# A GRU scan ahead of a mixture of experts: ScalarE makes s(1-z), VectorE's products and states become plain two-operand operations, and four instruction lists change

## The reference

```
def cell(h, x):
    gi = x @ W_ih + b_ih
    gh = h @ W_hh + b_hh
    i_r, i_z, i_n = jnp.split(gi, 3, axis=-1)
    h_r, h_z, h_n = jnp.split(gh, 3, axis=-1)
    r = jax.nn.sigmoid(i_r + h_r)
    z = jax.nn.sigmoid(i_z + h_z)
    n = jnp.tanh(i_n + r * h_n)
    h_new = (1.0 - z) * n + z * h
    return (h_new, h_new)
...
logits = flat_x @ Wg + bg
top_vals, top_idx = jax.lax.top_k(logits, TOPK)
...
for i in range(E):
    ...
    h = jax.nn.gelu(tok @ W1[i], approximate=False)
    y = h @ W2[i] * p
    out = out.at[sel_idx].add(y)
```

## Time and profile before

| | |
|---|---|
| median of 3 runs | 836.57 us (836.47 to 837.41) |
| the profiled execution's own time | 836.27 us |
| its span, first to last instruction | 834.5 us |
| TensorE busy in the span | 803.0 us, 96% |
| VectorE / ScalarE / GpSimd busy | 619.8 / 421.1 / 179.9 us |
| rough steps | from 61 to 174 us of the span |
| steps 24 to 71 | from 201 to 442 us |
| experts | from 488 us to the end |

### The profile page before, as it was taken

One profiled execution on the slowest core, in us unless ns is written; L12 is line 12 of the kernel. 1 busy time (PEld: TensorE's weight loads), 2 busy tenths in 40 slices (PEclk: granted clock), 3 DMA queues, 4 the chain that ended last, 5 costly groups with the idle time before them and its releaser, 6 DMA issues.

```text
span 834.5 us, 28320 instructions
## 1 busy us (share of the span) xinstructions
PE 803.0 (96%) x11781; PEld 528.0 (63%) x11782; DVE 619.8 (74%) x2113; ACT 421.1 (50%) x885; POOL 179.9 (22%) x459
## 2 busy tenths in 40 slices
PE   7999999999999999999995799999999999999996
PEld 3446556679999999999994444454445444444442
DVE  6979899878888888888888879767666676755300
ACT  0677666645566556554455448252835184417400
POOL 1002222123433334333330010121012101210011
PEclk9999999999999999999997899999999999999998
DMA  9810000000111010000001943471347224630022
GB/s 336 323 48 2 2 2 3 2 3 4 54 60 50 17 42 5 4 4 5 5 4 33 269 156 119 135 226 27 113 139 194 57 101 151 171 81 1 1 26 26
DMA packets 24286, 62.64 MB, mean 75 GB/s; under 512 B 4386, under 2 KB 4386, under 8 KB 22308
## 3 DMA queue, kind: packets, MB, share of 16 engines
q1 hardware_dynamic: 19312, 51.42, 18.1%
q0 software_dynamic: 3584, 8.42, 5.5%
q10 hardware_dynamic: 1268, 1.08, 0.4%
HBM read 52.50 MB, written 12.62 MB: 78 GB/s over the span
## 4 chain that ended last, share of the span: by engine, by line
PE 92%; DVE 5%; issue 1%; DMA 1%; ACT 0%; POOLq 0%; DVEq 0%
PE ps L459 29%; PE ps L666 20%; PE ps L680 20%; PE ps L451 10%; PE ps L469 3%; PE ps L434 3%; PE ps L424 2%; PE ps L600 1%; PE ps L653 1%; DVE big L1541 1%; PE ps L472 1%; DMA wa<-in_x_t 1%; DVE halves L1264 1%; DVE wa L1253 1%; PE ps L644 0%
## 5 line engine op out<-in xcount | busy, mean ns | idle before, releaser
L459 PE MATMUL ps<-halves,wa 128*128 128x64 f16 x8448 | 289.1, 193 | 1.4 <-DVE halves L1264 1.2
L459 PEld LDWEIGHTS ps<-halves,wa 128*128 128x128 f16 x8448 | 271.2, 98 | 20.2 <-DVE halves L1264 4.2
L680 PE MATMUL ps<-big 128*128 128x512 f16 x768 | 166.9, 379 | 0.0
L666 PE MATMUL ps<-hx,big 128*128 128x512 f16 x768 | 166.9, 379 | 0.0
L779 ACT ACTIVATE wa<-ps,un_gates 128x128 f32<-128x128 f32 x288 | 100.1, 365 | 111.0 <-PE ps L459 100.6
L680 PEld LDWEIGHTS ps<-big 128*128 128x128 f16 x768 | 75.1, 98 | 89.9
L666 PEld LDWEIGHTS ps<-hx,big 128*128 128x128 f16 x768 | 74.8, 98 | 90.0 <-issue 0.2
L784 ACT ACTIVATE wa<-wa,un_gates 128x64 f32<-128x64 f32 x288 | 97.4, 344 | 53.0 <-DVE wa L1253 48.9
L451 PE MATMUL ps<-hx,wb 128*128 128x512 f16 x432 | 106.9, 379 | 1.2 <-issue 1.1
L861 ACT ACTIVATE hx<-ps,un_hid_in 128x512 f32<-128x512 f32 x64 | 43.6, 682 | 109.2 <-PE ps L666 106.9
L1264 DVE SCALAR_TENSOR_TENSOR halves<-ocand,neg_scale,wa 128x64 f16<-128x64 f32 (+1 forms) x288 | 80.6, 280 | 4.4 <-issue 0.5
(11 more groups left out here) (221 smaller groups left out, 791.4 us busy)
## 6 DMA issues: line engine op xcount, KB each, us to landing
wa<-in_w SPq DMA_DIRECT2D x28, 1024.0 KB, 5.2
hs_rows<-big SPq DMA_DIRECT2D x8, 512.0 KB, 6.3
big<-in_w_hh SPq DMA_DIRECT2D x4, 768.0 KB, 19.6
wb<-in_w SPq DMA_DIRECT2D x12, 256.0 KB, 2.6
big<-in_w_ih SPq DMA_DIRECT2D x2, 1024.0 KB, 12.5
hx<-in_x_t SPq DMA_DIRECT2D x2, 1024.0 KB, 16.5
big<-in_w_ih ACTq DMA_DIRECT2D x2, 512.0 KB, 6.6
wa<-in_x_t SPq DMA_DIRECT2D x2, 512.0 KB, 6.2
```

The costliest lines, as they stand in the source:

```text
L459: mm = pe.matmul(gate_ps[:, j, g, :], whh_parts[:, k, w, (4 * g + j) * P:(4 * g + j + 1) * P], halves[:, src, k, h, :], start=False, stop= ...
L666: mm = pe.matmul(ps[:, m % 2, :], w1p[:, w, k, m * P:(m + 1) * P], tokT[:, t, k, :], start=(k == 0 and n == 0), stop=(k == KD - 1 and n == 2))
L680: mm = pe.matmul(ps[:, 2 + g % 2, :], hid[:, h, k, g * P:(g + 1) * P], w2p[:, w, k, :], start=(k == 0 and n == 0), stop=(k == KH - 1 and n ...
```

## The change

ScalarE gets four new instructions a step, `kept_of(j)`: Identity with scale -s and bias s, out of z, so `wz` = s(1-z). `one_less_z(j)` is now wz x candidate, and `blend` and `keep_state` are ocand + z h, with no column operand. `one_less_z` waits for two semaphores, `tanh_done` and `wz_done`, instead of one. The candidate is written over its input (`cand = cand_in`), and the room goes to `wz`. The lists of TensorE, ScalarE, GpSimd and VectorE's exact steps are new; VectorE's rough list stays.

```diff
-        cand = gru_tmp(KD * COLS).rearrange("p (j c) -> p j c", j=KD)
+        cand = cand_in
+        wz = gru_tmp(KD * COLS).rearrange("p (j c) -> p j c", j=KD)
...
-        ORDER = ((INJECT, 0, 0), (INJECT, 1, 0), (HIGH, 1, 0), (INJECT, 2, 0), (HIGH, 0, 0), (HIGH, 2, 0),
...
+        ORDER = ((INJECT, 0, 0), (INJECT, 1, 0), (INJECT, 2, 0), (HIGH, 1, 0), (HIGH, 2, 0), (HIGH, 0, 0), (HIGH, 1,
...
-                for f, j in ((sig, 0), (sig, 1), (sig, 2), (tanh, 0), (tanh, 1), (sig, 3), (tanh, 2), (tanh, 3)):
+
+                def kept_of(j):
+                    act.wait_ge(S["sig_done"], base + j + 1)
+                    act.activation(wz[:, j, :], rz[:, j, 1, :], ACT.Identity, bias=scale[:, STATE:STATE + 1],
+                                   scale=neg_scale[:, 0:1]).then_inc(S["wz_done"], 1)
+
+                for f, j in ((sig, 0), (sig, 1), (kept_of, 0), (sig, 2), (tanh, 0), (tanh, 1), (kept_of, 1), (sig, 3),
+                             (tanh, 2), (kept_of, 2), (kept_of, 3), (tanh, 3)):
...
-                for j in range(KD):
-                    carry(j)
-                if low:
-                    for j in range(POOL_LOWS):
-                        low_part(j)
+                exact = ((carry, 0), (carry, 1), (carry, 2), (low_part, 0), (carry, 3), (low_part, 1))
+                rough = ((carry, 0), (carry, 1), (carry, 2), (carry, 3))
+                for f, j in exact if low else rough:
+                    f(j)
...
                     dve.wait_ge(S["tanh_done"], base + j + 1)
-                    dve.scalar_tensor_tensor(ocand[:, j, :], rz[:, j, 1, :], -1.0, cand[:, j, :],
-                                             ALU.add, ALU.mult).then_inc(S["ocand_done"], 1)
+                    dve.wait_ge(S["wz_done"], base + j + 1)
+                    dve.tensor_tensor(ocand[:, j, :], wz[:, j, :], cand[:, j, :], ALU.mult).then_inc(S["ocand_done"], 1)
...
-                    dve.scalar_tensor_tensor(high_of(j), old(ocand_, j), neg_scale[:, 0:1], old(zh_, j),
-                                             ALU.mult, ALU.add).then_inc(S["high_ready"], 1)
+                    dve.tensor_tensor(high_of(j), old(ocand_, j), old(zh_, j), ALU.add).then_inc(S["high_ready"], 1)
...
-                    dve.scalar_tensor_tensor(after(j), old(ocand_, j), neg_scale[:, 0:1], old(zh_, j),
-                                             ALU.mult, ALU.add).then_inc(S["state_done"], 1)
+                    dve.tensor_tensor(after(j), old(ocand_, j), old(zh_, j), ALU.add).then_inc(S["state_done"], 1)
...
-                exact = ((reset, 0), (candidate_in, 0), (reset, 1), (candidate_in, 1), (reset, 2),
-                         (one_less_z, 0), (candidate_in, 2), (blend, 0), (keep_state, 0), (one_less_z, 1),
-                         (reset, 3), (blend, 1), (candidate_in, 3), (one_less_z, 2), (keep_state, 1), (blend, 2),
-                         (one_less_z, 3), (keep_state, 2), (blend, 3), (keep_state, 3), (low_part, 2),
-                         (low_part, 3))
+                exact = ((reset, 0), (reset, 1), (candidate_in, 0), (candidate_in, 1), (reset, 2), (one_less_z, 0),
+                         (candidate_in, 2), (blend, 0), (one_less_z, 1), (keep_state, 0), (blend, 1), (reset, 3),
+                         (keep_state, 1), (candidate_in, 3), (one_less_z, 2), (blend, 2), (one_less_z, 3),
+                         (keep_state, 2), (blend, 3), (keep_state, 3), (low_part, 2), (low_part, 3))
```

More of the change, by code:

```diff
@@ L239, in gru_moe @@
              gi_mm gi_high gi_low gi_kept diag_ready sig_done gates_known gi_known x_known wih_high wih_split whh_high x_high x_split peak_ready peak_known chain whh_ready zh_done warmed high_ready state_done low_ready last_low_ready gates_mm rn_done
-            candin_ready tanh_done ocand_done start_saved check_a worst_ready worst_mm flag_ready
+            candin_ready tanh_done wz_done ocand_done start_saved check_a worst_ready worst_mm flag_ready
             gru_over turned bhn_clear bhn_loaded bhn_split wg_split lg_mm lg_kept sq_done probs_in probs_stored group_made rows_copied rows_stored steps_made exp_in exp_done
@@ L274, in gru_moe @@
         INJECT = 2
-        ORDER = ((INJECT, 0, 0), (INJECT, 1, 0), (HIGH, 1, 0), (INJECT, 2, 0), (HIGH, 0, 0), (HIGH, 2, 0),
[L276 to L280, removed]
+        ORDER = ((INJECT, 0, 0), (INJECT, 1, 0), (INJECT, 2, 0), (HIGH, 1, 0), (HIGH, 2, 0), (HIGH, 0, 0), (HIGH, 1,
+                 1), (HIGH, 2, 1), (LOW, 0, 0), (LOW, 2, 0), (HIGH, 0, 1), (LOW, 1, 0), (INJECT, 3, 0), (LOW, 1, 1),
+                 (HIGH, 1, 2), (HIGH, 0, 2), (HIGH, 0, 3), (LOW, 0, 1), (LOW, 0, 2), (LOW, 0, 3), (LOW, 1, 3), (LOW,
+                 1, 2), (HIGH, 1, 3), (LOW, 2, 3), (HIGH, 2, 3), (HIGH, 2, 2), (LOW, 2, 1), (LOW, 2, 2), (HIGH, 3,
+                 3), (HIGH, 3, 0), (LOW, 3, 1), (HIGH, 3, 1), (LOW, 3, 0), (HIGH, 3, 2), (LOW, 3, 3), (LOW, 3, 2))
         FILLS = (13, 2, 2, 1)
```

## The result

| | before | changed |
|---|---|---|
| median | 836.96 us (4 runs) | 849.81 us (849.66 to 850.72, 4 runs) |
| ratio to before | 1 | 1.0156 (95% interval 1.0140 to 1.0172) |
| span of the profiled execution | 834.5 us | 848.2 us |
| `sig(0)` of step 20 | 174.07 us | 175.59 us |
| step 24 to step 71, 47 steps | 236.05 us | 247.43 us |

The change makes the kernel 1.6% slower; the forecast was 849.0 us. The 13.7 us of span split into 11.4 in steps 24 to 71, 1.5 before step 20, 0.3 in steps 20 to 23 and 0.5 behind step 71. The moment of the first `sig(0)` differs by up to 1.2 us between traces, so the rough steps are better compared from there: steps 0 to 19 take 112.88 us before and 114.60 with the change, 1.7 more. The 0.5 us at the end lies within the spread of that part over the traces (397.1 to 398.6 us, e7 aside).

A forecast was written before the change was run, and what follows sets the result against it. The scan was taken to run just above TensorE's floor, bound by the path from `sig(0)` to `blend(0)`. The second path lengthens each of 47 steps by 0.27 us, 12.7 us on 836.27: 849.0 us, range 832 to 856.

The forecast's parts named there:

- The stall before the first HIGH: TensorE's wait for `blend(0)`'s high part at a step's start, 0.1 to 0.2 us; the change would remove it.
- the second path: Chain through `one_less_z(1)` to `low_part(3)` and the next `sig(0)`: nearly as long today, 5.35 us worked with the change.
- The price of `kept_of`: On ScalarE, 0.43 us each at a pitch of 0.34; VectorE's `one_less_z` then waits 0.10 behind it.
- The collisions: VectorE instructions starting just after a GpSimd start take 0.11 us longer; four a step, 0.33 us together.
- GpSimd's `low_part` starts 0.14 behind the end of its `keep_state`: Block 0's low part at 2.80 us after `sig(0)`, `keep_state(1)` 0.11 after it, hence a collision.
- the sum of all four: Step worked with all four collisions: 5.35 us, against 5.02 without any; three quarters taken, giving 5.27.
- the 4.22 us: TensorE's time for a step's 144 matmuls of line 459, at a pitch of about 29.3 ns.
- Rough steps do not move: Steps 0 to 19 would stay as now, since a 0.8 us cover before a high part's first use hides `kept_of`.
- TensorE as the bound: Rival: collisions fall elsewhere, `kept_of` is as cheap as `tanh`, steps reach TensorE's floor, 830.7 us; chance 0.22.
- The plain instructions are not shorter: Half of the last rival: VectorE's forms without column operands save nothing; 0.45 us a step, 857.4 us; chance 0.10.
- the one on the shared interface: Rule that GpSimd and VectorE share an SBUF interface, so VectorE instructions with two SBUF inputs contend; trace agreed partly.
- The halved throughput of the three-operand shape: Rule favouring the change: some 0.07 us more gained for each of 12 VectorE instructions; today's trace disagreed.

The follow-up runs named there:

- e7: Changed kernel with GpSimd's two low_part operations left out from step 21 on: 1281.38 us, with further rounds run; 5.12 us a step in the first 72 steps.
- e3: Changed kernel with TensorE's old list alone put back: 856.72 us.
- e6: Changed kernel with `kept_of` taking constants (scale -128, bias 128, function Copy) in place of two column operands: 840.66 us.
- e11: Changed kernel with the old operations (no `kept_of`, column operands) kept in steps 0 to 18: 848.74 us.
- e10: Changed kernel with `kept_of` taking constants and lists laid out for its shorter time; holds only for inputs whose scale is 128: 830.63 us.
- e1: Changed kernel with GpSimd's old list alone put back (all four carries, then the two low parts): 843.00 us.
- e4: Kernel before, given the new lists of TensorE, VectorE and GpSimd but keeping the old operations: 856.86 us.
- e8: Changed kernel's operations with four other lists, found by exchanging entries and working each out: 834.19 us.

## Why the prediction was right, and where it was not

**The stall before the first HIGH is gone, at the price of the second path: shown.** The after trace has next to no wait there (0.02 us, 0.13 before), e3 brings one of 0.35 back, and the waits now lie where the prediction put them: ahead of the units with high part 2 (0.12), high part 3 (0.11) and low part 3 (0.10). All waits went from 0.17 to 0.42 us a step, and the step grew by as much.

**The price of `kept_of`: right.** 429 ns against 0.43, and a wait of 0.10 behind it (289.20 + 0.43 to 289.73), both read from forms of the kernel before. e6 shows what it is worth. The 0.10 is not the price of every instruction with two waits, though: `one_less_z(0)`, which has two as well, starts 0.03 behind `tanh(0)`.

**The collisions: right in kind, one of four wrong.** `candidate_in(0)`, `candidate_in(3)` and `one_less_z(2)` collide. `keep_state(1)` does not: the step "GpSimd's `low_part` starts 0.14 behind the end of its `keep_state`" failed, since for block 0 it starts 0.07 behind it (289.88 + 0.22 to 290.17), and then `keep_state(1)` starts 0.17 behind GpSimd, which costs nothing. I had taken the sum of all four, 5.35; 5.24 came out. Of the 0.11 between them, `keep_state(1)` is 0.11, and `one_less_z(1)` came 0.05 earlier than worked out (2.25 after `sig(0)`, not 2.30), while the two late collisions cost 0.12 to 0.14 each in place of 0.11. The forecast had cut the part of the four collisions by a quarter for doubt. The cut had no mechanism behind it, and the nearness of 849.0 to 849.81 owes something to it, and something to the next point: that is luck. One sum is off as well: 88 matmuls in 2.78 - 0.19 us have a pitch of 29.8 ns, not 29.3, since that row holds a short wait for low part 3; single pitches where nothing waits average 29.3, so the 4.22 us stand.

**"Rough steps do not move": wrong, by 1.7 us.** I read the cover of 0.8 us from a plain rough step. In steps with extra tiles and splits it is smaller, and `kept_of` shows. e11 took it all back. The 47 steps gave 11.4 us where I had 12.7; this error and that one nearly cancel.

**The rivals.** TensorE as the bound did not occur, but e10 reached it, at 830.63 us against the 830.7 worked out: of the kernels run, only the one with both a cheap `kept_of` and other lists. "The plain instructions are not shorter" fell (225 and 219 ns). Of the two rules of the Trainium skill weighed there, the one on the shared interface (GPSIMD Engine Reference, 1 Specifications) agrees with e1, e4 and e7, though only where the VectorE instruction starts just behind GpSimd's. The halved throughput of the three-operand shape (Vector Engine (DVE) Microarchitecture Reference, 7 Points that are easy to get wrong) is not seen next to the two-operand shape: the plain `one_less_z` averages 227 ns in e8, the old one 220 in before.

## What to carry to other kernels

Where several engines work from hand-written lists with steps of a few us, an operation has no price of its own: the same new operations gained 7 us under one set of lists and lost 8 under another, and with lists fitted to each set they drew. Work a whole step out from starts, pitches and semaphore delays of the trace, check the working against today's step, and only then judge an edit. Take the cover of hidden work from its worst step, not from a plain one. Where an engine's rows are merged, look at the pitch inside them: here every us that the kernels differ by in the exact steps lay there.
